# The order of PE's and ScalarE's steps within a chunk of an embedding tower: copies, within-double slots and layers moved

## The chip, the cores and the metric

One core of one Trainium2 chip runs the whole program in one launch. The metric is the device time in microseconds of one execution; of the kernel before three runs are at hand, and one further execution was recorded by the hardware profiler.

## The reference

For 2048 rows, 32 categorical fields are looked up in 32 tables (64 numbers each). Every pair of fields (496 pairs) goes through a bilinear form of its own, the 496 results through a linear layer of 256, and that with 16 dense numbers through three more layers:

```python
rows, cols = np.triu_indices(num_fields, k=1)
p = feat_emb[:, rows, :]
q = feat_emb[:, cols, :]
pij = jnp.einsum('bpe,dpe,bpd->bp', p, kernel, q)
z = pij @ W.T + b
h = jnp.concatenate([z, dense_ctx], axis=1)
h = jnp.maximum(h @ W_top1 + b_top1, 0.0)
h = jnp.maximum(h @ W_top2 + b_top2, 0.0)
y = h @ W_top3
```

All of it is float32.

## The kernel before, in words

The 2048 rows are worked on in four chunks of 512 columns (`CHUNKS`, numbered 0 to 3). The fields are taken two at a time as 16 "doubles": a double is 2 fields x 64 numbers = 128 partitions. `emb_t` holds the 16 doubles of one chunk, transposed, so that a row of the batch is a column.

GpSimd (POOL) gathers the table rows by indirect DMAs, eight for each double and chunk (L420). What PE (TensorE) does is written as one list of steps, `program()` (L202 to L233), which every engine walks through for its own part. The kinds of steps are:

- **turn** (L650): PE transposes gathered doubles into `bilinear` in PSUM; ScalarE (ACT) copies them to `emb_t` (L464, `turn_out`). From chunk 1 on two doubles are turned at a time. `TURNS` says after which slot of the chunk, `TURNS_EARLY` after which slot of the chunk before.
- **slot** (L669, 92 a chunk): the kernels of one double m against one double j times the columns of double m: 8 matmuls on quarter-height, half-width pieces of the array that work side by side (16 records in the profile, since a float32 matmul has two). VectorE (DVE) multiplies the result by double j (L575) into `prod`. Four slots of a chunk, `(3, None)`, `(7, None)`, `(11, None)` and `(15, None)`, hold the pairs *within* four doubles; their product takes four narrow instructions on DVE (L572). Here they are called within slots. They stand at the end of rows 3, 7, 11 and 15, that is as slots 6, 21, 44 and 91.
- **batch** (L685, 32 a chunk, a double m of 6 to 13 and a tile of 128 rows): the same with the batch on the partitions. DVE multiplies (L586) into `batch_prod`, a ring of 3, and ACT reduces it in two halves (**reduce**, L497 to L508), each half 8 ACTIVATE instructions with an accumulator read (L505). The halves are queued on ACT `REDUCE_LAG` = 2 and 4 steps behind their batch.
- **sum** (L710, 46 "quads" a chunk, each of two slots): PE adds the products over partitions into `sums`. Quads 0 to 31 are group 0, the rest group 1. After quad 31 ACT copies group 0 out of `sums` to `sums_sb` (`group_out`, L475), and quad 32 must wait for that copy (L715). **join** (L699) adds the reduced batches to group 1 at the chunk's end, which ACT copies too; then SyncE (SP) fetches the dense inputs into spare rows of `sums_sb` by 8 DMAs (L390).
- **layer** (L727, 7 a chunk): outputs 0 to 3 of the first dense layer (4 terms each; the linear layer of 256 has been folded into its weights), 4 and 5 of the second, 6 of the last. A term is one 128x128 weight block against 512 columns. ACT copies each with its bias and ReLU (L486, L490, L493). Layers of chunk i run amid the slots of chunk i+1: after slot 10 and every fourth slot behind it (`FIRST_LAYER`, `LAYER_EVERY`). Those of chunk 3 run at the very end.

PSUM has eight banks. Two hold `sums`; the other six are a ring of three pairs, `bilinear`. Slots, batches, turns and layers use a pair each in the order of the list; a step has to wait until the pair of the third use before it was read out by DVE or ACT (`ring_free`, L635). Batches run from slot 11 on, every 2.3 slots (chunk 0: from 17). In chunk 0, which has no layers, a double is turned two units ahead of its first use.

What PE, DVE and ACT each do within a chunk is thus fixed by one list, in which a step may stand behind others on its own engine that wait for something else.

## Time and profile before

| | |
|---|---|
| median of 3 runs | 823.51 us (820.65 to 825.17) |
| the profiled execution, its own time | 825.15 us |
| span of its instructions | 823.4 us |
| PE busy | 772.7 us (94%) |
| DVE busy | 623.8 us (76%) |
| ACT busy | 552.4 us (67%) |
| POOL busy | 472.0 us (57%), over by 630 us |
| mean granted TensorE clock | 0.99 |

A chunk is told by its steps: the first slot of chunks 0 to 3 starts on PE at 45.9, 213.8, 409.0 and 600.3 us, and the last slot of chunk 3 at 786.0 us. A row of the timeline merges instructions of one line that follow each other without a gap: its start, its length, and in brackets how long the engine stood idle before it and what ended that. Matmuls overlap, so the distance from one row's start to the next one's start is what a step costs, and the length is not.

### The profile page before, as it was taken

How to read it: one execution, taken by the hardware profiler on the slowest of the kernel's cores; microseconds unless marked ns; L12 is line 12 of the kernel's file. 1: busy time of each engine (PE TensorE's matmuls, PEld its weight loads, DVE VectorE, ACT ScalarE, POOL GpSimd, SP SyncE). 2: the span in 40 equal slices, each digit the busy share in tenths (PEclk: the TensorE clock that was granted, in tenths of full speed). 3: DMA queues.
4: the chain of work that ended last, by engine and by line, in shares of the span. 5: the costliest groups of instructions: out<-in, count | busy, mean ns of one | idle time of the engine just before them, and what ended most of it. 6: DMA issues, size and time to landing. Idle time of an engine off the chain costs nothing.

```text
span 823.4 us, 29630 instructions
## 1 busy us (share of the span) xinstructions
PE 772.7 (94%) x11784; PEld 284.5 (35%) x11784; DVE 623.8 (76%) x580; ACT 552.4 (67%) x4181; POOL 472.0 (57%) x502
## 2 busy tenths in 40 slices
PE   4988899999999999989999999998999999998978
PEld 1323233434333333333433333333343333332333
DVE  4487899999755669989866758997885568997930
ACT  0112799999616588999614768999813668999911
POOL 5777777777777777777777777777774000000000
PEclk9999999999999999999999999999999999999999
DMA  9911111111111111111111111111110000000000
GB/s 260 358 41 29 28 30 28 30 29 29 30 30 28 28 29 28 30 29 30 28 31 27 29 28 30 29 30 28 30 30 19 2 2 2 3 3 2 3 3 0
DMA packets 21681, 30.50 MB, mean 37 GB/s; under 512 B 10898, under 2 KB 11410, under 8 KB 20904
## 3 DMA queue, kind: packets, MB, share of 16 engines
q0 software_dynamic: 15872, 16.28, 10.3%
q1 hardware_dynamic: 3512, 9.58, 3.3%
q10 hardware_dynamic: 2160, 2.76, 1.3%
q8 instruction: 92, 1.51, 0.8%
q14 instruction: 45, 0.37, 0.2%
HBM read 28.58 MB, written 0.01 MB: 35 GB/s over the span
## 4 chain that ended last, share of the span: by engine, by line
PE 69%; ACT 11%; POOL 7%; DVE 6%; issue 5%; DMA 2%; SPq 0%; DVEq 0%; POOLq 0%
PE bilinear L679 27%; PE sums L721 14%; PE bilinear L747 11%; PE bilinear L693 10%; ACT batch_prod L505 10%; POOL emb L420 5%; PE bilinear L656 3%; DVE prod L572 3%; PE bilinear L610 2%; POOL emb_first L420 2%; DVE prod L575 2%; DMA sums_sb<-looked_ids 1%; DVE w_comb_sb L555 1%; PE sums L705 1%; DMA emb<-table,ids_sb 1%
## 5 line engine op out<-in xcount | busy, mean ns | idle before, releaser
L505 ACT ACTIVATE batch_prod<-batch_prod 128x64 f32<-128x64 f32 x2048 | 489.6, 243 | 21.2 <-DVE batch_prod L586 21.1
L575 DVE TENSOR_TENSOR prod<-bilinear,emb_t 128x1024 f32<-128x1024 f32 x352 | 415.9, 1218 | 81.4 <-PE bilinear L679 79.8
L420 POOL DMA_INDIRECT emb<-table,ids_sb x368 | 347.3, 944 | 112.1 <-issue 110.3
L505 ACT ACTIVATION_READ_ACCUMULATOR batch_prod<-batch_prod 128x1 f32 x2048 | 387.3, 189 | 0.0
L679 PE MATMUL bilinear<-emb_t,k_sb 64*32 64x512 f32 x5888 | 371.7, 595 | 6.8 <-DVE prod L572 4.8
L721 PE MATMUL sums<-prod,row_sel 64*32 64x512 f32 x2944 | 199.3, 596 | 9.8 <-ACT sums_sb L475 8.1
L586 DVE TENSOR_TENSOR batch_prod<-bilinear,emb_first 128x1024 f32<-128x1024 f32 x128 | 156.1, 1219 | 52.7 <-PE bilinear L693 51.7
L679 PEld LDWEIGHTS bilinear<-emb_t,k_sb 64*32 64x32 f32 x5888 | 108.5, 106 | 204.2 <-issue 137.7
L420 POOL DMA_INDIRECT emb_first<-table,ids_sb x128 | 124.1, 969 | 44.7 <-issue 37.6
L693 PE MATMUL bilinear<-k_sb,emb_t 64*32 64x512 f32 x2048 | 139.9, 601 | 0.0
L464 ACT ACTIVATE emb_t<-bilinear 128x1024 f32<-128x1024 f32 (+1 forms) x40 | 33.9, 848 | 97.8 <-PE bilinear L656 91.2
L721 PEld LDWEIGHTS sums<-prod,row_sel 64*32 64x32 f32 x2944 | 56.1, 108 | 116.1 <-issue 94.7
L747 PE MATMUL bilinear<-sums_sb,w_comb_sb 128*128 128x512 f32 x128 | 58.6, 603 | 7.1 <-DVE prod L572 4.4
L693 PEld LDWEIGHTS bilinear<-k_sb,emb_t 64*32 64x32 f32 x2048 | 40.4, 108 | 69.2 <-issue 52.3
L572 DVE TENSOR_TENSOR prod<-bilinear,emb_t 64x512 f32<-64x512 f32 x64 | 44.1, 689 | 10.2 <-PE bilinear L679 8.5
L486 ACT ACTIVATE h_sb<-bilinear,b_comb_sb 128x512 f32<-128x512 f32 x16 | 11.0, 688 | 59.3 <-PE bilinear L747 59.3
L747 PEld LDWEIGHTS bilinear<-sums_sb,w_comb_sb 128*128 128x128 f32 x128 | 23.2, 189 | 42.5 <-issue 28.1
L656 PE MATMUL bilinear<-ident,emb 128*128 128x128 f32 x184 | 26.3, 281 | 7.9 <-DMA emb<-table,ids_sb 6.4
L475 ACT ACTIVATE sums_sb<-sums 128x512 f32<-128x512 f32 x16 | 8.6, 587 | 33.7 <-PE sums L705 33.7
L610 PE MATMUL bilinear<-prod,batch_prod 100*32 100x512 f32 (+1 forms) x160 | 20.1, 668 | 11.8 <-DVE prod L541 11.8
L656 PEld LDWEIGHTS bilinear<-ident,emb 128*128 128x128 f32 x184 | 19.6, 141 | 31.9 <-DVE prod L575 11.5
L747 PE MATMUL bilinear<-h_sb,w_sb 128*128 128x512 f32 x64 | 29.3, 603 | 0.9 <-ACT h_sb L486 0.9
(29 smaller groups left out, 105.3 us busy)
## 6 DMA issues: line engine op xcount, KB each, us to landing
emb<-table,ids_sb POOLq DMA_INDIRECT x368, 2.5
emb_first<-table,ids_sb POOLq DMA_INDIRECT x128, 2.5
k_sb<-k_slots SPq DMA_DIRECT2D x2, 896.0 KB, 19.8
k_sb<-k_slots SPq DMA_DIRECT2D x1, 1600.0 KB, 23.1
k_sb<-k_slots SPq DMA_DIRECT2D x1, 1408.0 KB, 19.4
k_sb<-k_slots SPq DMA_DIRECT2D x1, 1088.0 KB, 16.8
sums_sb<-looked_ids SPq DMA_DIRECT2D x1, 1024.0 KB, 9.6
k_sb<-k_slots SPq DMA_DIRECT2D x1, 1024.0 KB, 26.5
```

The source lines that it names most:

```text
L420: nc.gpsimd.indirect_dma_start(fields_of(i, j, t)[:, f % 2, :], None, tables[f], bass.IndirectOffsetOnAxis(ap=ids_sb[:, start + t, f:f + 1 ...
L464: nc.scalar.activation(emb_t[:, j:j + several, 0:n], bilinear[:, bank:bank + several, 0:n], ACT.Copy).then_inc(s_emb_t, 1)
L505: last = nc.scalar.activation(products, products, ACT.Copy, accum_out=batch_sums[:, t, half, row + f:row + f + 1])
L572: last = nc.vector.tensor_tensor(prod[rows, at + half, 0:n], bilinear[rows, bank + half, 0:n], emb_t[by, double, 0:n], ALU.mult)
L575: last = nc.vector.tensor_tensor(prod[:, at:at + 2, 0:n], bilinear[:, bank:bank + 2, 0:n], emb_t[:, j:j + 1, 0:n].to_broadcast([P, 2, n]), ...
L586: nc.vector.tensor_tensor(batch_prod[:, use % BATCH_PRODS, :, :], bilinear[:, bank:bank + 2, :], first.to_broadcast([P, 2, COLS]), ALU.mul ...
L610: last = nc.tensor.matmul(bilinear[col:col + QUARTER, bank, :], tables_sb[0:parts, f, k, e:e + QUARTER], one_hot[0:parts, n % ONE_HOT_RING ...
L656: last = nc.tensor.transpose(bilinear[:, bank + n, t * P:(t + 1) * P], fields_of(i, j + n, t), ident[:])
L679: last = nc.tensor.matmul(bilinear[col:col + QUARTER, bank + row // EMB, 0:n], k_sb[row:row + EMB, operand, col:col + QUARTER], emb_t[row: ...
L693: last = nc.tensor.matmul(bilinear[col:col + QUARTER, bank + row // EMB, :], emb_t[row:row + EMB, m, t * P + col:t * P + col + QUARTER], k ...
L721: last = nc.tensor.matmul(sums[32 * b:32 * b + 32, half, 0:n], row_sel[rows, 31 - pos:63 - pos], prod[rows, at + b, 0:n], start=pos == 0, ...
L747: last = nc.tensor.matmul(bilinear[0:weights.shape[1], ring_bank("layer", i, k), 0:n], weights, x, start=term == 0, stop=term == LAYER_TER ...
```

## The change

The code of the steps stays, and so do their numbers: no slot, batch, sum or transpose is added or taken away. What changes:

- Within slots stand at places 4, 21, 38 and 88 of a chunk.
- In `program()` sums due now are queued ahead of reductions due now, and reductions are held back while the last quad of a group is about to come (`copy_near`). `REDUCE_LAG` is 3.
- Places of turns and batches: `TURNS`, `TURNS_EARLY`, `BATCH_FROM`. Layers of the chunk before stand after slots 5, 8, 18, 21, 25, 34 and 38 instead of 10, 14, 18, 22, 26, 30 and 34.
- A layer waits for each term's input by itself, not for all of them before the first.
- The layers of the last chunk no longer use the ring: each has a bank of its own, and the first two terms of outputs 0 to 3 (they need group 0 alone) are a step `begin` of their own, ahead of the terms that need group 1 and the dense inputs.

```diff
+WITHIN_PLACES = {3: 4, 7: 21, 11: 38, 15: 88}
+SLOTS = [(m, j) for m, j in OPERANDS if j is not None and (m not in BATCHED_ROWS_OF or j not in BATCH_DOUBLES)]
+for _m, _place in WITHIN_PLACES.items():
+    SLOTS.insert(_place, (_m, None))
...
-FIRST_LAYER = 10
-LAYER_EVERY = 4
-REDUCE_LAG = 2
-TURNS_EARLY = {84: 0, 87: 2, 90: 4}
-TURNS = {8: 6, 17: 8, 27: 10, 40: 12, 54: 14}
-FIRST_BATCH_FROM, FIRST_BATCH_EVERY = 17, 2.3
-BATCH_FROM, BATCH_EVERY = 11, 2.3
+REDUCE_LAG = 3
+REDUCE_HOLD = 1
+TURNS_EARLY = {82: 0, 88: 2, 91: 4}
+TURNS = {8: 6, 21: 8, 26: 10, 38: 12, 59: 14}
+LAYERS = (5, 8, 18, 21, 25, 34, 38)
+FIRST_BATCH_FROM, FIRST_BATCH_EVERY = 20, 2.2
+BATCH_FROM, BATCH_EVERY = 10, 2.3
+BEGUN_TERMS = HALVES
...
-        while reduces and reduces[0][0] <= at:
+        while sums and sums[0][0] <= at:
+            step = sums.pop(0)[1]
+            if step[0] == "join":
+                steps += [r for _, r in reduces if r[1] == step[1]]
+                reduces = [r for r in reduces if r[1][1] != step[1]]
+            steps.append(step)
+        copy_near = any(due <= at + REDUCE_HOLD and kind == "sum" and (n + 1) % GROUP_QUADS == 0
+                        for due, (kind, _, n) in sums)
+        while reduces and reduces[0][0] <= at and not copy_near:
             steps.append(reduces.pop(0)[1])
-        while sums and sums[0][0] <= at:
-            steps.append(sums.pop(0)[1])
     steps += [step for at, step in reduces] + [step for at, step in sums]
-    steps += [("layer", NCHUNKS - 1, k) for k in range(NOUTS)]
+    steps += [("begin", NCHUNKS - 1, k) for k in range(H1_OUTS)] + [("layer", NCHUNKS - 1, k) for k in range(NOUTS)]
...
+        def layer_bank(i, k):
+            return bilinear[:, k % (2 * RING) if i == NCHUNKS - 1 else ring_bank("layer", i, k), :]
...
+            def begin(i, k):
+                if k == 0:
+                    pe.wait_ge(s_prod, NCHUNKS * NSLOTS)
+                    pe.wait_ge(s_batch_prod, BATCHES_TO[NCHUNKS])
+                layer_terms(i, k, range(0, BEGUN_TERMS))
...
+            def layer_terms(i, k, terms):
+                n = cols(i)
+                for term in terms:
                     if k < H1_OUTS:
+                        pe.wait_ge(s_sums_out, i * NSUMS + term + 1)
                         if term == NSUMS - HALVES:
                             pe.wait_ge(s_dense, (i + 1) * (16 * 8))
...
                     elif k < H2_OUTS:
+                        pe.wait_ge(s_layer_out, i * NOUTS + term + 1)
```

Three places of the order, before and with the change. In the changed kernel the lines are other ones: L699 is the slot, L713 the batch, L741 the sum, L725 the join, L676 the turn, L783 a layer's term; on ACT L525 is the reduction, L484 the copy of a turn, L495 of a group, L506, L510 and L513 of a layer.

ACT in chunk 1, from the copy of layer output 6 of the chunk before (before: L493) to the copies after the join (before: L475 the second time); eight ACTIVATEs are one half reduction. Before:

```order
57 L493 ACTIVATE h_sb<-bilinear 1x512
58 L505 ACTIVATE batch_prod,batch_sums<-batch_prod 128x64 x40
59 L464 ACTIVATE emb_t<-bilinear 128x1024
60 L505 ACTIVATE batch_prod,batch_sums<-batch_prod 128x64 x96
61 L464 ACTIVATE emb_t<-bilinear 128x1024
62 L505 ACTIVATE batch_prod,batch_sums<-batch_prod 128x64 x96
63 L475 ACTIVATE sums_sb<-sums 128x512 x2
64 L505 ACTIVATE batch_prod,batch_sums<-batch_prod 128x64 x120
65 L464 ACTIVATE emb_t<-bilinear 128x1024
66 L505 ACTIVATE batch_prod,batch_sums<-batch_prod 128x64 x8
```

and with the change:

```order
52 L484 ACTIVATE emb_t<-bilinear 128x1024
53 L513 ACTIVATE h_sb<-bilinear 1x512
54 L525 ACTIVATE batch_prod,batch_sums<-batch_prod 128x64 x144
55 L484 ACTIVATE emb_t<-bilinear 128x1024
56 L525 ACTIVATE batch_prod,batch_sums<-batch_prod 128x64 x48
57 L495 ACTIVATE sums_sb<-sums 128x512 x2
58 L525 ACTIVATE batch_prod,batch_sums<-batch_prod 128x64 x112
59 L484 ACTIVATE emb_t<-bilinear 128x1024
60 L525 ACTIVATE batch_prod,batch_sums<-batch_prod 128x64 x32
```

Between the turn of doubles 14 and 15 and the copy of group 0, ACT has 6 half reductions instead of 12; behind the copy, up to the turn of doubles 0 and 1 of the next chunk, 14 instead of 15.

PE at the start of chunk 1, from the join of chunk 0 to its first layer. Before:

```order
154 L705 MATMUL sums<-ident,batch_sums 32x128 x32
155 L679 MATMUL bilinear<-emb_t,k_sb 32x512 x8
156 L721 MATMUL sums<-prod,row_sel 32x512 x8
157 L679 MATMUL bilinear<-emb_t,k_sb 32x512 x16
158 L721 MATMUL sums<-prod,row_sel 32x512 x8
159 L679 MATMUL bilinear<-emb_t,k_sb 32x512 x8
160 L656 MATMUL bilinear<-ident,emb 128x128 x8
161 L679 MATMUL bilinear<-emb_t,k_sb 32x512 x8
162 L721 MATMUL sums<-prod,row_sel 32x512 x8
163 L679 MATMUL bilinear<-emb_t,k_sb 32x512 x8
164 L747 MATMUL bilinear<-sums_sb,w_comb_sb 128x512 x4
```

and with the change:

```order
155 L725 MATMUL sums<-ident,batch_sums 32x128 x32
156 L699 MATMUL bilinear<-emb_t,k_sb 32x512 x8
157 L783 MATMUL bilinear<-sums_sb,w_comb_sb 128x512 x4
158 L741 MATMUL sums<-prod,row_sel 32x512 x8
159 L699 MATMUL bilinear<-emb_t,k_sb 32x512 x16
160 L741 MATMUL sums<-prod,row_sel 32x512 x8
161 L699 MATMUL bilinear<-emb_t,k_sb 32x512 x8
162 L676 MATMUL bilinear<-ident,emb 128x128 x8
163 L783 MATMUL bilinear<-sums_sb,w_comb_sb 128x512 x4
```

The first layer output stands one slot behind the join, where it stood eight steps and a turn behind; the second stands directly behind the turn.

PE at the end of the program, after the join of chunk 3, with what each instruction waits for. Before:

```order
1606 L747 MATMUL bilinear<-sums_sb,w_comb_sb 128x512 [waits s_sums_out,s_prod]
1607 L747 MATMUL bilinear<-sums_sb,w_comb_sb 128x512
1608 L747 MATMUL bilinear<-sums_sb,w_comb_sb 128x512 [waits s_dense]
1609 L747 MATMUL bilinear<-sums_sb,w_comb_sb 128x512
```

and with the change:

```order
1606 L783 MATMUL bilinear<-sums_sb,w_comb_sb 128x512 [waits s_sums_out,s_batch_prod,s_prod]
1607 L783 MATMUL bilinear<-sums_sb,w_comb_sb 128x512 [waits s_sums_out] x7
1608 L783 MATMUL bilinear<-sums_sb,w_comb_sb 128x512 [waits s_dense,s_sums_out]
1609 L783 MATMUL bilinear<-sums_sb,w_comb_sb 128x512 [waits s_sums_out]
```

Eight terms of group 0, two of each of four outputs, now stand ahead of the first term that waits for the dense inputs, instead of two.

## Rows read from the trace of the kernel before

**Rows 1.** The page: the span and the busy time of the engines
```profile
span 823.4 us, 29630 instructions
PE 772.7 (94%) x11784; PEld 284.5 (35%) x11784; DVE 623.8 (76%) x580; ACT 552.4 (67%) x4181; POOL 472.0 (57%) x502
```

**Rows 2.** Timeline of PE around quad 32 of chunk 1
```profile
361.47 1.06 PE L721 MATMUL sums<-prod,row_sel 64*32 64x512 f32 x16
...
364.05 1.06 PE L679 MATMUL bilinear<-emb_t,k_sb 64*32 64x512 f32 x16
367.64 1.09 PE L721 MATMUL sums<-prod,row_sel 64*32 64x512 f32 x16 [2.53 <-ACT sums_sb L475]
368.52 1.62 PE L679 MATMUL bilinear<-emb_t,k_sb 64*32 64x512 f32 x16
...
372.79 1.50 PE L679 MATMUL bilinear<-emb_t,k_sb 64*32 64x512 f32 x24
```

**Rows 3.** The timeline's group copy on ACT, and a run of reductions in the chain
```profile
366.53 1.05 ACT L475 ACTIVATE sums_sb<-sums 128x512 f32<-128x512 f32 x2
...
103.03 11.46 ACT batch_prod L505 x96
```

**Rows 4.** Windows: length, busy PE, PEld, DVE, ACT, POOL; clock; DMA
```profile
369.00:372.00 3.00, 3.00 (x40) 1.08 (x32) 1.23 (x1) 3.00 (x27) 2.39 (x3) 0.50 0.18 38
244.77:397.56 152.79, 147.74 (x2300) 53.00 (x2292) 122.56 (x110) 127.94 (x1005) 115.33 (x123) 0.99 0.15 29
```

**Rows 5.** Timeline around within slots 21 and 44, chunk 1, PE and DVE
```profile
267.85 1.06 PE L679 MATMUL bilinear<-emb_t,k_sb 64*32 64x512 f32 x16
270.31 3.70 PE L747 MATMUL bilinear<-sums_sb,w_comb_sb 128*128 128x512 f32 x8 [1.40 <-DVE prod L572]
...
325.84 1.09 PE L679 MATMUL bilinear<-emb_t,k_sb 64*32 64x512 f32 x16 [1.12 <-DVE prod L572]
...
267.46 2.80 DVE L572 TENSOR_TENSOR prod<-bilinear,emb_t 64x512 f32<-64x512 f32 x4
```

**Rows 6.** Timeline of PE from the join of chunk 1 to slot 11
```profile
415.43 1.96 PE L705 MATMUL sums<-ident,batch_sums 128*32 128x128 f32 x64
417.32 1.09 PE L679 MATMUL bilinear<-emb_t,k_sb 64*32 64x512 f32 x16
...
426.66 1.07 PE L679 MATMUL bilinear<-emb_t,k_sb 64*32 64x512 f32 x16
427.66 3.70 PE L747 MATMUL bilinear<-sums_sb,w_comb_sb 128*128 128x512 f32 x8
431.29 1.09 PE L679 MATMUL bilinear<-emb_t,k_sb 64*32 64x512 f32 x16
```

**Rows 7.** Timeline of PE: chunk 0, its join, start of chunk 1
```profile
101.77 0.63 PE L656 MATMUL bilinear<-ident,emb 128*128 128x128 f32 x4 [0.55 <-DMA emb<-table,ids_sb]
...
115.06 1.95 PE L679 MATMUL bilinear<-emb_t,k_sb 64*32 64x512 f32 x32 [0.60 <-ACT emb_t L464]
...
221.19 1.07 PE L705 MATMUL sums<-ident,batch_sums 128*32 128x128 f32 x31
...
231.53 0.66 PE L656 MATMUL bilinear<-ident,emb 128*128 128x128 f32 x4 [1.54 <-DMA emb<-table,ids_sb]
...
240.17 1.09 PE L679 MATMUL bilinear<-emb_t,k_sb 64*32 64x512 f32 x16
```

**Rows 8.** Timeline after the last slot: PE, and SP's queue
```profile
791.51 1.95 PE L705 MATMUL sums<-ident,batch_sums 128*32 128x128 f32 x64
794.76 1.95 PE L747 MATMUL bilinear<-sums_sb,w_comb_sb 128*128 128x512 f32 x4 [1.30 <-ACT sums_sb L475]
798.17 12.28 PE L747 MATMUL bilinear<-sums_sb,w_comb_sb 128*128 128x512 f32 x28 [1.45 <-DMA sums_sb<-dense_t]
819.30 1.88 PE L747 MATMUL bilinear<-sums_sb,w_sb 128*1 128x512 f32 x4 [0.87 <-ACT sums_sb L490]
...
794.65 2.30 SPq L390 DMA_DIRECT2D sums_sb<-dense_t  x8
```

More of the change, by code:

```diff
@@ L221, in program @@
                 steps.append(("turn", i + 1, (TURNS_EARLY[which], 2)))
-            k = (which - FIRST_LAYER) // LAYER_EVERY
-            if i > 0 and (which - FIRST_LAYER) % LAYER_EVERY == 0 and 0 <= k < NOUTS:
-                steps.append(("layer", i - 1, k))
+            if i > 0 and which in LAYERS:
+                steps.append(("layer", i - 1, LAYERS.index(which)))
         else:
             reduces += [(at + REDUCE_LAG * (half + 1), ("reduce", i, (*which, half))) for half in range(HALVES)]
-        while reduces and reduces[0][0] <= at:
+        while sums and sums[0][0] <= at:
[7 more added lines that the diff above has]
+        while reduces and reduces[0][0] <= at and not copy_near:
             steps.append(reduces.pop(0)[1])
-        while sums and sums[0][0] <= at:
-            steps.append(sums.pop(0)[1])
     steps += [step for at, step in reduces] + [step for at, step in sums]
-    steps += [("layer", NCHUNKS - 1, k) for k in range(NOUTS)]
+    steps += [("begin", NCHUNKS - 1, k) for k in range(H1_OUTS)] + [("layer", NCHUNKS - 1, k) for k in range(NOUTS)]
     return steps
 PROGRAM = program()
-RING_USES = [step for step in PROGRAM if step[0] in ("slot", "batch", "turn", "layer")]
+RING_USES = [step for step in PROGRAM
+             if step[0] in ("slot", "batch", "turn") or (step[0] == "layer" and step[1] < NCHUNKS - 1)]
 RING_USE = {step: n for n, step in enumerate(RING_USES)}
@@ L479, in layer_out @@
                 n = cols(i)
-                source = bilinear[:, ring_bank("layer", i, k), 0:n]
+                source = layer_bank(i, k)[:, 0:n]
                 act.wait_ge(s_layer, i * NOUTS + k + 1)
@@ L765, in _ @@
                     join(i)
+                elif kind == "begin":
+                    begin(i, which)
                 elif kind == "layer":
```

22 lines of the change are left out of this document (11 added, 11 removed).

## The prediction

> **What bounds the kernel now.** I read the page first, for the busy shares: PE is busy in 772.7 of 823.4 us [rows 1]. Work that only shifts between DVE and ACT gains nothing, and PE's own work does not change in number. So the question is how much of PE's time is waiting, and which of it goes. For that I read PE's timeline start to start. Three consecutive steps take 364.05 - 361.47 = 2.58 us, 0.86 us each, if nothing waits [rows 2]; slots, batches and sums cost all the same. Whatever a step takes beyond that is a wait, and the bracket names who ended it. The places priced below make some 9 us of such waits in a steady chunk. The timelines of ACT and DVE there show why they are so costly. A half reduction takes 11.46 / 6 = 1.91 us (16 instructions of 96), so a batch costs ACT 3.82 us [rows 3]. A batch comes every 2.3 slots, which cost PE 3.3 + 1.15 steps = 3.82 us. DVE needs 3.3 x 1.13 = 3.7 us for it, at the 1.13 us from product to product that the timeline shows and of which the narrow within product is the exception, 2.80 us [rows 5]. Where no layer lies between, the three engines are equal, and no delay of one is made good. Over the batches of chunk 1 ACT is busy in 127.94 of 152.79 us [rows 4].
>
> **The change part by part.** All gains are of PE's time, against the profiled execution (span 823.4, its own time 825.15 us, 1.6 above the median 823.51, well inside 820.65 to 825.17).
>
> *Copy of group 0.* Quad 32 starts at 367.64 instead of 364.05 + 0.86: 2.73 us [rows 2]. ACT reached the copy only at 366.53, for 12 half reductions stood ahead of it, though quad 31 was done near 362.5. The next three steps take 372.79 - 368.52 = 4.27 instead of 2.57 us: 1.70 us more [rows 2], and the granted clock there is 0.50, the 1.2 GHz level, after PE had stood idle 2.53 us [rows 4]. Together 4.43 us, in chunks 1, 2 and 3. With the change 6 half reductions stand ahead. I count in us from the start of the turn of doubles 12 and 13 (slot 38). PE: turn and layer 6 until 3.0, 41 steps, turn of 14 and 15 done at 39.4, then 14 steps, quad 31 done at 51.5, quad 32 due at 54.0. ACT: copy of layer 6 done at 3.6, 18 halves to 38.0, waits for the turn, its copy to 40.4, 6 halves to 51.9, group copy (1.05) to 53.0. It is in time by 1.0 us. Gain 3 x 4.43 = **13.3 us**. Late next is ACT: 14 halves to 79.7, the copy of doubles 0 and 1 to 80.7, and PE wants that bank at 80.9. The ring of 3 `batch_prod` buffers holds by the same count, by 0.1 to 1 us in each batch. So ACT lives with margins of tenths; what it costs lies between 0 and the 2.73 us given back in each chunk.
>
> *Within slots.* Before, the 2.80 us on DVE hit the third ring use behind: 270.31 - 267.85 - 1.00 = 1.46 us at slot 21, and 1.33 us at slot 44, of which the timeline brackets 1.12 as idle [rows 5]. At 21 and 38 a turn and a layer (1.05 + 3.63 or 1.9 us) now follow, on which DVE has nothing to do, and the third use comes after them. Gain 3 x 2.8 = **8.4 us**. For (15, None) at 88 the turn behind covers it but for 0.35 us at slot 90, about what slot 2 of the next chunk waited before: nothing. (3, None) lies under the layer behind the join.
>
> *Turn directly ahead of a layer.* A step ahead of a layer takes 1.00 instead of 0.86, and one behind it 0.88 [rows 6]. Three layers a chunk (8, 21, 38) now share that with a turn: 3 x 3 x 0.17 = **1.5 us**.
>
> *Layer 0 one slot behind the join.* It needs the dense inputs, which SP can fetch only once ACT has copied the join. At the end of the program they take from the join's start 798.17 - 791.51 = 6.66 us until PE goes on [rows 8]. With the change PE gets there after join 1.89, slot 0.86 + 0.14 and two terms 1.79 = 4.67 us: **a new wait of 2.0 us**. It hides the 0.42 us that sum 0 waited for the copy and DVE's backlog from the within slot. Before, slot 11 began 431.29 - 415.43 = 15.86 us behind the join [rows 6]; now the same steps end at 6.66 + 1.99 (two terms and restart) + 5 steps + turn 1.2 + 3 steps = 16.7. Loss 0.85 us in chunks 2 and 3: **-1.7 us**. The Trainium skill (DMA: Bandwidth & Descriptors, Anatomy of one DMA) gives a DMA a fixed cost of about 2.0 us; behind the last of eight issues [rows 8], which ends at 796.95, that would be 798.9, and the new wait 2.8 us. The row has 1.2 us there, and the sum goes by it.
>
> *Chunk 0 and start of chunk 1.* Until 101.77 PE waits for gathers [rows 7], at POOL's pace, so nothing is won. Behind it the changed order has one batch more to do (5 instead of 6 done). ACT had the turn of double 11 late (until 115.06 [rows 7], 0.83 us), and similar ones later, 2.7 us in all. In chunk 0 ACT is the bound: 57 halves from 103.0, 108.9, and 6.3 for copies end at 218.2, with its idle at double 11 about 219.3. Then the join, before at 221.19: **+1.8 us**. From there chunk 1 took 240.17 - 221.19 = 18.98 to slot 11, with a gather wait at 231.53 and the clock down behind it; now 16.7, as the turn comes at 232.5, after the gather: **+2.3 us**. If the join comes no earlier only the first goes.
>
> *End.* `begin` can start at 793.4, when the join's matmuls are out, instead of 794.76 + a wait to 798.17. 8 + 8 terms of 0.86 end at 807.2, before at 798.17 + 12.1 = 810.3 [rows 8]. Waiting term by term, output 4 needs no pause for the copy of output 3 (1.05 us), and the last layer's first term runs under the copy of output 5 (0.87). Sum 3.1 + 1.0 + 0.8 = **4.9 us**. The extra waits cost nothing: 28 records with a wait at every second term run without a gap, 0.43 us each [rows 8]. DVE ends chunk 3 as before: the same work stands behind slot 86.
>
> Sum: 13.3 + 8.4 + 1.5 - 1.7 + 1.8 + 2.3 + 4.9 = 30.5 us. From this I take 1.5 us for ACT's thin margins, towards the low end of 0 to 3 x 2.73, because the count fits everywhere. Gain 29.0: span 794.4, median 823.5 - 29.0 = **794.5 us**.
>
> **The rivals.**
> 1. *The wait moves.* ACT used the 4.4 us stall to catch up: it was 3 us behind before, and even after. If ACT arrives later at slot 38 than I count, or a half takes longer beside full DVE, the 2.73 us come back at the turn of doubles 0 and 1 or at the `batch_prod` ring, with the clock's 1.70. For it: margins of 0.1 us. Against: ACT idles 25 of 152.79 us [rows 4], most of it before slot 38. Given back whole, 13.3: 807.8 us.
> 2. *The new wait lowers the clock.* 2.0 us behind the join, where the array runs small matmuls, in three chunks. Behind idle 2.53 us the clock fell [rows 2, 4]; behind 1.40 it did not [rows 5]. Each fall costs 1.70 us as above: 3 x 1.7, so 799.6 us. The Trainium skill (TensorE: Matmul & The Clock Gate, Part 1) says the same, that idleness takes PE to half clock, and speaks against placing a wait there. At the program's end rows show the like, 1.30 and 1.45 us idle [rows 8], with terms behind at full pace.
> 3. *Slower: ACT becomes the bound of every chunk.* The place is the turn of doubles 0 and 1, at slot 82, after 38 halves since slot 38. To lose 30.5 us and more ACT must come 10 us too late in each of three chunks. That is 0.27 us on each half, 2.18 instead of 1.91 us; it decides from there. Then PE waits 10.5 us a chunk there, some 825 us, and 828 with the clock's falls. The halves are longer nowhere in the trace, though DVE and PE are full beside them.
> 4. *The order does not do what it says*: the reductions held back pile up ahead of the join. Against: the order shows them done by the third slot behind the last batches. It would cost 2 x 1.91 us a chunk: 806 us.
>
> **How the numbers follow.** My forecast has 0.60, with its own range 791 to 798. Rival 1 has 0.17 (800 to 810, as it may come in part), rival 2 0.14 (796 to 801), rival 4 0.04, rival 3 0.03; 0.02 is left for more gain than I count. The range reaches from 790.5, with no margin lost and a bit more from chunk 0, to 806, with most of rival 1. About 0.5% (4 us) is what a measurement of this kernel can tell from none. Only rival 3 is not faster by more: faster 0.95, same 0.02, slower 0.03.
>
> **What would show it.** Quad 32 three steps behind quad 31 with no bracket; no 0.50 clock in chunks 1 to 3; layers behind within slots starting without idle; a bracket of about 2 us for the dense DMA in each of three layers 0; one row of 16 terms at the end, the last layer 5 us nearer to the last slot. A first-slot-to-first-slot distance of 184 us in chunk 2, instead of 191.3, is right, 188 or more is wrong (rival 1), and brackets that name ACT at slot 84 or DVE's batch products say where.

## The result, and the profile after

The changed kernel takes 798.68 us (median of 6 runs, 796.73 to 799.11), the kernel before 823.55 us in the same session (6 runs, 820.65 to 825.17). The ratio is 0.9694, with a 95% interval from 0.9673 to 0.9716: faster by 24.9 us. Forecast were 794.5 us, within 790.5 to 806.0.

The profiled execution of the changed kernel was its fastest, 796.73 us. The page, beside [rows 1]:

```profile
span 794.9 us, 29641 instructions
PE 760.8 (96%) x11784; PEld 283.7 (36%) x11784; DVE 623.9 (78%) x580; ACT 551.3 (69%) x4181; POOL 472.3 (59%) x502
```

The work is the same, the span 28.5 us shorter. From profile to profile more was won than from median to median: the profiled execution of before lay 1.6 us above its median and that of after 1.95 us below. From join to join the profiles compare as follows. A chunk is counted from the join before it to its own; the end is what follows the join of chunk 3.

| | before | after | gain | forecast |
|---|---|---|---|---|
| start to join of chunk 0 | 221.2 | 222.5 | -1.3 | +1.8 |
| chunk 1 | 194.24 | 184.22 | 10.0 | 10.0 |
| chunk 2 | 191.28 | 184.03 | 7.25 | 6.9 |
| chunk 3 | 184.80 | 177.45 | 7.35 | 6.9 |
| end | 31.84 | 26.74 | 5.1 | 4.9 |

The forecasts by chunk are the prediction's terms added up where they fall: 4.43 + 2.8 + 0.5 + 2.3 for chunk 1, and 4.43 + 2.8 + 0.5 - 0.85 for chunks 2 and 3. They make 30.5 us; the 1.5 us of margin taken off stood in no chunk. From first slot to first slot chunk 2 took 184.0 us (400.6 to 584.6), the number that the prediction had named as its sign of being right.

**Quad 32.** The timeline of PE in chunk 1 of the changed kernel, from quad 31 (the first row) to quad 32 (the fourth), beside [rows 2]:

```profile
357.05 1.06 PE L741 MATMUL sums<-prod,row_sel 64*32 64x512 f32 x16
357.91 1.06 PE L713 MATMUL bilinear<-k_sb,emb_t 64*32 64x512 f32 x16
358.77 1.92 PE L699 MATMUL bilinear<-emb_t,k_sb 64*32 64x512 f32 x32
360.49 1.06 PE L741 MATMUL sums<-prod,row_sel 64*32 64x512 f32 x16
361.34 1.06 PE L713 MATMUL bilinear<-k_sb,emb_t 64*32 64x512 f32 x16
```

From start to start it is 3.44 us, four steps of 0.86: no wait, no bracket, and the granted clock from 357 to 362 us is 1.00. The distance was 367.64 - 361.47 = 6.17 us, with the same four steps.

**Within slots.** The timeline of PE around slot 21 of chunk 1, beside [rows 5]:

```profile
264.73 1.06 PE L699 MATMUL bilinear<-emb_t,k_sb 64*32 64x512 f32 x16
265.73 1.09 PE L676 MATMUL bilinear<-ident,emb 128*128 128x128 f32 x8
266.66 3.60 PE L783 MATMUL bilinear<-sums_sb,w_comb_sb 128*128 128x512 f32 x8
270.19 1.09 PE L699 MATMUL bilinear<-emb_t,k_sb 64*32 64x512 f32 x16
```

Turn, layer and next slot follow each other without idle; DVE's 2.8 us lie under them. The pair is also cheaper than the prediction counted. The turn takes 266.66 - 265.73 = 0.93 us and the layer behind it 270.19 - 266.66 = 3.53, where they take 1.02 and 3.63 apart; with the shared 0.17 that makes 0.36 us a pair instead of 0.17, at slots 8 and 21. It is most of the 0.4 us by which chunks 2 and 3 gained more than forecast.

**Layer 0.** The timeline of PE behind the join of chunk 0:

```profile
222.49 1.95 PE L725 MATMUL sums<-ident,batch_sums 128*32 128x128 f32 x64 [0.67 <-ACT batch_prod L525]
224.37 1.09 PE L699 MATMUL bilinear<-emb_t,k_sb 64*32 64x512 f32 x16
225.39 1.98 PE L783 MATMUL bilinear<-sums_sb,w_comb_sb 128*128 128x512 f32 x4
229.52 1.95 PE L783 MATMUL bilinear<-sums_sb,w_comb_sb 128*128 128x512 f32 x4 [2.14 <-DMA sums_sb<-dense_t]
231.40 1.09 PE L741 MATMUL sums<-prod,row_sel 64*32 64x512 f32 x16
```

The new wait is there, 2.14 us (1.84 and 1.98 in the next two chunks). With it the three chunks lose 2.59, 2.29 and 2.43 us on the layer beyond its bare terms. Of each of these 0.21 us are no wait: a layer that waits for nothing takes 3.63 us instead of 4 x 0.86. The clock did not fall behind this wait (window: length, busy PE, PEld, DVE, ACT, POOL; clock; DMA):

```profile
230.00:232.00 2.00, 2.00 (x20) 0.71 (x26) 0.00 (x0) 0.49 (x1) 1.39 (x3) 1.00 0.13 25
```

**End.** The timeline of PE from the join of chunk 3, beside [rows 8]:

```profile
768.19 1.95 PE L725 MATMUL sums<-ident,batch_sums 128*32 128x128 f32 x64
770.08 14.00 PE L783 MATMUL bilinear<-sums_sb,w_comb_sb 128*128 128x512 f32 x32
783.91 7.03 PE L783 MATMUL bilinear<-h_sb,w_sb 128*128 128x512 f32 x16
790.87 1.88 PE L783 MATMUL bilinear<-sums_sb,w_sb 128*1 128x512 f32 x4
```

Sixteen terms in one row of 32 records and no bracket: the dense inputs come while PE works on what needs none of them.

**Chunk 0** went the other way. Its timeline shows waits of PE behind the within slots at 38 and 88, where this chunk has no layer:

```profile
120.15 1.09 PE L699 MATMUL bilinear<-emb_t,k_sb 64*32 64x512 f32 x16 [1.27 <-DVE prod L592]
...
210.95 1.09 PE L713 MATMUL bilinear<-k_sb,emb_t 64*32 64x512 f32 x16 [0.86 <-DVE prod L592]
```

and ACT's timeline shows that ACT, which I had taken as the bound of this chunk, stands idle ahead of its copy of group 0 (the queue rule holds its reductions back there):

```profile
169.09 1.08 ACT L495 ACTIVATE sums_sb<-sums 128x512 f32<-128x512 f32 x2 [1.37 <-PE sums L741]
```

Even so ACT is the last at the end of this chunk: in the timeline above, the join at 222.49 us waits 0.67 us for a reduction of ACT.

### The profile page after: what moved, and what is told of

It is laid out like the page before. It is cut to its first block, busy times and chain, and to the rows that moved or that the text cites. A ratio compares the mean times of both kernels' runs of the same rounds, so it can differ in the third digit from the quotient of the medians.

```text
span 794.9 us, 29641 instructions
## 1 busy us (share of the span) xinstructions
PE 760.8 (96%) x11784; PEld 283.7 (36%) x11784; DVE 623.9 (78%) x580; ACT 551.3 (69%) x4181; POOL 472.3 (59%) x502
## 3 DMA queue, kind: packets, MB, share of 16 engines
q8 instruction: 92, 1.51, 0.8%
## 4 chain that ended last, share of the span: by engine, by line
PE 72%; POOL 9%; issue 6%; DVE 5%; ACT 5%; DMA 1%; SPq 1%; DVEq 0%; POOLq 0%
PE bilinear L699 30%; PE sums L741 16%; PE bilinear L713 12%; PE bilinear L783 11%; POOL emb L440 5%; ACT batch_prod L525 5%; POOL emb_first L440 4%; PE bilinear L676 3%; DVE prod L595 3%; DVE prod L592 1%; DVE batch_prod L606 1%; PE sums L725 1%; SPq L410 1%; DMA sums_sb<-dense_t 1%; ACT emb_t L484 0%
## 5 line engine op out<-in xcount | busy, mean ns | idle before, releaser
L525 ACT ACTIVATE batch_prod<-batch_prod 128x64 f32<-128x64 f32 x2048 | 489.2, 244 | 17.6 <-DVE batch_prod L606 17.6
L525 ACT ACTIVATION_READ_ACCUMULATOR batch_prod<-batch_prod 128x1 f32 x2048 | 389.9, 190 | 0.0
L699 PE MATMUL bilinear<-emb_t,k_sb 64*32 64x512 f32 x5888 | 368.1, 594 | 4.3 <-DVE prod L592 3.4
L741 PE MATMUL sums<-prod,row_sel 64*32 64x512 f32 x2944 | 196.8, 590 | 0.7 <-DVE prod L595 0.7
L699 PEld LDWEIGHTS bilinear<-emb_t,k_sb 64*32 64x32 f32 x5888 | 110.0, 107 | 207.1 <-issue 151.0
L713 PE MATMUL bilinear<-k_sb,emb_t 64*32 64x512 f32 x2048 | 137.1, 590 | 1.1 <-DVE prod L592 1.1
L484 ACT ACTIVATE emb_t<-bilinear 128x1024 f32<-128x1024 f32 (+1 forms) x40 | 34.0, 851 | 96.7 <-PE bilinear L676 90.0
L741 PEld LDWEIGHTS sums<-prod,row_sel 64*32 64x32 f32 x2944 | 55.9, 107 | 99.5 <-issue 92.0
L783 PE MATMUL bilinear<-sums_sb,w_comb_sb 128*128 128x512 f32 x128 | 58.5, 600 | 6.0 <-DMA sums_sb<-dense_t 6.0
L713 PEld LDWEIGHTS bilinear<-k_sb,emb_t 64*32 64x32 f32 x2048 | 39.0, 107 | 69.8 <-issue 48.8
L506 ACT ACTIVATE h_sb<-bilinear,b_comb_sb 128x512 f32<-128x512 f32 x16 | 11.0, 687 | 56.4 <-PE bilinear L783 56.4
L783 PEld LDWEIGHTS bilinear<-sums_sb,w_comb_sb 128*128 128x128 f32 x128 | 23.0, 190 | 36.5 <-issue 33.8
L676 PE MATMUL bilinear<-ident,emb 128*128 128x128 f32 x184 | 26.6, 284 | 3.9 <-DMA emb<-table,ids_sb 3.9
L676 PEld LDWEIGHTS bilinear<-ident,emb 128*128 128x128 f32 x184 | 19.9, 142 | 27.5 <-issue 12.6
L783 PE MATMUL bilinear<-h_sb,w_sb 128*128 128x512 f32 x64 | 29.2, 602 | 0.0
L495 ACT ACTIVATE sums_sb<-sums 128x512 f32<-128x512 f32 x16 | 8.6, 588 | 25.7 <-PE sums L725 24.3
```

Of the source, the lines that this page charges most:

```text
L484: nc.scalar.activation(emb_t[:, j:j + several, 0:n], bilinear[:, bank:bank + several, 0:n], ACT.Copy).then_inc(s_emb_t, 1)
L525: last = nc.scalar.activation(products, products, ACT.Copy, accum_out=batch_sums[:, t, half, row + f:row + f + 1])
L676: last = nc.tensor.transpose(bilinear[:, bank + n, t * P:(t + 1) * P], fields_of(i, j + n, t), ident[:])
L699: last = nc.tensor.matmul(bilinear[col:col + QUARTER, bank + row // EMB, 0:n], k_sb[row:row + EMB, operand, col:col + QUARTER], emb_t[row: ...
L713: last = nc.tensor.matmul(bilinear[col:col + QUARTER, bank + row // EMB, :], emb_t[row:row + EMB, m, t * P + col:t * P + col + QUARTER], k ...
L741: last = nc.tensor.matmul(sums[32 * b:32 * b + 32, half, 0:n], row_sel[rows, 31 - pos:63 - pos], prod[rows, at + b, 0:n], start=pos == 0, ...
```

## The experiments

**My theory** after the result: each part works as its term says; the order of ACT's queue removes quad 32's wait; the within slots' places, the layer's wait and `begin` are worth their terms; and chunk 0 lost because ACT is its bound and the batches begin three slots later. **The rivals**: the turn of doubles 14 and 15, moved from slot 54 to 59, removes quad 32's wait, and the queue rule does nothing; the clock falls behind layer 0's wait in most executions, so that the wait costs more than its length; chunk 0 lost to the within slots.

The twelve runs were made in three sessions, on three chips. Where a run is compared with the changed kernel's 798.68 us, that number is from the session of the result; the kernel before, within 0.3 us of the same median in the second and third session, is the link.

### First session: one part at a time

On the first chip the kernel before itself took 1339.5 us instead of 823.5. PE stands there waiting on nothing that the profile shows, as long as POOL gathers. The windows of the first experiment, before and after the last gather (it ends near 1090 us; columns as in [rows 4]):

```profile
792.80:1089.00 296.20, 255.97 (x2365) 85.94 (x2362) 124.39 (x112) 119.38 (x881) 121.68 (x129) 0.85 0.08 16
1132.00:1312.00 180.00, 174.97 (x2804) 63.53 (x2796) 146.13 (x133) 134.14 (x1040) 0.00 (x0) 1.00 0.01 3
```

Chunk 3, which lies behind the gathers, runs there as it does elsewhere, so I read chunk 3 of these four profiles alone, against 184.80 us of before and 177.45 us of after.

*The queue rule alone*, put on the kernel before, with its turns, within slots, layers and end:

```diff
-REDUCE_LAG = 2
+REDUCE_LAG = 3
+REDUCE_HOLD = 1
...
-        while reduces and reduces[0][0] <= at:
-            steps.append(reduces.pop(0)[1])
         while sums and sums[0][0] <= at:
...
+        copy_near = any(due <= at + REDUCE_HOLD and kind == "sum" and (n + 1) % GROUP_QUADS == 0
+                        for due, (kind, _, n) in sums)
+        while reduces and reduces[0][0] <= at and not copy_near:
+            steps.append(reduces.pop(0)[1])
```

> The kernel before with the new queue rule alone (sums ahead of reductions, reductions held back near a group's last quad, lag 3): in chunks 1 to 3 ACT has 10 half reductions instead of 12 between the turn of doubles 14 and 15 and the group copy. Theory A (the two halves taken from ahead of the copy are what removes the wait of quad 32): the copy starts 2 x 1.91 = 3.8 us earlier, near 362.7, just when quad 31 is done; quad 32 does not wait, the clock does not fall behind it: 3 x 4.43 = 13.3 us less, about 810 us. Theory B (ACT is behind as a whole, so that the wait moves to the next turn): quad 32 free, but a wait of 2 to 3 us ended by ACT at the turn of doubles 0 and 1: about 818 us.

Measured: 1340.57 us, ratio 1.0 (0.9956 to 1.0044), which says nothing on this chip. Chunk 3 took 180.33 us, 4.47 less than before, against the 4.43 that the prediction gave the term. Between the turn and the group copy this order has 10 half reductions, not 6, and quad 32 does not wait. So the rule suffices by itself.

*The rule off*, in the changed kernel:

```diff
-REDUCE_LAG = 3
-REDUCE_HOLD = 1
+REDUCE_LAG = 2
+REDUCE_HOLD = 0
...
-        while reduces and reduces[0][0] <= at and not copy_near:
+        while reduces and reduces[0][0] <= at:
             steps.append(reduces.pop(0)[1])
+        while sums and sums[0][0] <= at:
+            steps.append(sums.pop(0)[1])
```

> The changed kernel with the queue rule undone (reductions ahead of sums, no holding back, lag 2), all places of the change kept: 6 half reductions still stand between the turn of doubles 14 and 15 and the group copy, but 19 instead of 18 ahead of that turn. Theory A (the rule removes the wait of quad 32): the wait of 2.73 us and the clock's 1.70 us come back in chunks 1 to 3, about 812 us. Theory C (the later turn of doubles 14 and 15, at slot 59 instead of 54, does it, since ACT no longer idles 1.85 us ahead of it): ACT's copy of the turn is 0.5 us later, the group copy ends 0.5 us ahead of quad 32, no wait: 799 us within 1.5.

Measured: 1321.53 us, ratio 0.9867 (0.979 to 0.9944). Chunk 3 took 177.34 us, as with the rule, and quad 32 did not wait. So beside the other changes the rule does nothing in chunk 3.

*The turn alone*, in the kernel before:

```diff
-TURNS = {8: 6, 17: 8, 27: 10, 40: 12, 54: 14}
+TURNS = {8: 6, 17: 8, 27: 10, 40: 12, 59: 14}
```

> The kernel before with one number changed: doubles 14 and 15 are turned after slot 59 instead of 54. Theory A (the queue rule alone matters): as before, 823.5 us. Theory C: ACT does not idle 1.85 us ahead of that turn, the group copy comes 1.85 us earlier in chunks 1 to 3, quad 32 waits 0.9 instead of 2.73 us and the clock may stay up: 3 x 1.85 = 5.5 us, and 3 x 1.70 = 5.1 us if it does, 813 us (818 if it falls all the same).

Measured: 1341.75 us, ratio 1.0012 (0.9965 to 1.0059). Chunk 3 took 181.27 us, 3.53 less; from quad 31 to quad 32 it is 4.34 us, of which 0.9 is a wait. The later turn removes most of the wait too, and the clock's fall with it. Both parts do the same thing, and they do not add.

*The within slots back*, in the changed kernel:

```diff
-WITHIN_PLACES = {3: 4, 7: 21, 11: 38, 15: 88}
+WITHIN_PLACES = {3: 6, 7: 21, 11: 44, 15: 91}
```

> The changed kernel with the within slots back at 6, 21, 44 and 91. My sum gave 1.33 us for slot 44 in each of chunks 1 to 3 and nothing for 6 and 91; slot 21 keeps its place beside turn and layer. So 4 us slower, 802.7 us, with an idle of about 1.1 us ended by DVE two uses behind slot 44. Rival (the wait given to DVE's backlog at slots 88 and 4 in the changed kernel, 0.45 to 1.1 us, is worth as much): about as the changed kernel, 799 us. Chunk 0 should gain 1.5 us at slot 38, where no layer covers the within slot, if ACT is not the bound there.

Measured: 1317.7 us, ratio 0.9862 (0.9795 to 0.9928). Chunk 3 took 179.6 us, 2.15 more. It lost 1.92 us at quad 44, behind the within slot at its very end, where the changed kernel lost 0.75 + 0.92 us at slot 90 and quad 44, and five pieces of 0.3 to 0.7 us around the other two. Of the new places, these three are tried; slot 21 keeps its place in both kernels.

### Second session: the end, layer 0, and chunk 0

The kernel before took 823.28 us on this chip (7 runs, 821.97 to 824.19).

*No `begin`*, in the changed kernel:

```diff
-    steps += [("begin", NCHUNKS - 1, k) for k in range(H1_OUTS)] + [("layer", NCHUNKS - 1, k) for k in range(NOUTS)]
+    steps += [("layer", NCHUNKS - 1, k) for k in range(NOUTS)]
...
-                    terms = range(BEGUN_TERMS, LAYER_TERMS[k])
+                    if k == 0:
+                        pe.wait_ge(s_prod, NCHUNKS * NSLOTS)
+                        pe.wait_ge(s_batch_prod, BATCHES_TO[NCHUNKS])
+                    terms = range(LAYER_TERMS[k])
```

> The changed kernel without the begin steps: the last chunk's layers do all four terms of an output before the next; the waits term by term stay. Theory (my sum): the dense inputs land 6.66 us behind the join's start, PE has two terms (1.79 us) to do until then and waits about 2.8 us instead of none: 3.0 us slower than the changed kernel, 801.7 us. Rival (the gain at the end comes from waiting term by term and from the join's copy no longer being waited for by all terms): the same as the changed kernel within 1 us.

Measured: 802.90 us, ratio 0.9757 (0.9738 to 0.9776). The end took 29.8 us instead of 26.74, 3.06 more. The forecast was 3.0 us more than the changed kernel, 801.7. Its timeline:

```profile
770.50 1.95 PE L725 MATMUL sums<-ident,batch_sums 128*32 128x128 f32 x64
772.38 1.98 PE L786 MATMUL bilinear<-sums_sb,w_comb_sb 128*128 128x512 f32 x4
777.20 12.26 PE L786 MATMUL bilinear<-sums_sb,w_comb_sb 128*128 128x512 f32 x28 [2.83 <-DMA sums_sb<-dense_t]
```

The wait of 2.83 us is back ahead of the 28 records. The other 5.1 - 3.06 = 2.0 us of the end's gain stay without `begin`: they come from the waits term by term and the banks of their own, which this kernel keeps; the two were not taken apart. By medians it is 4.2 us slower. In its profile chunk 1 took 186.00 us, 1.8 more than in that of after, with the clock down in layer 0 behind 2.11 us of idle (clock 0.53 over the window from 229.7 to 233.3 us).

*Layer 0 later*, in the changed kernel:

```diff
-LAYERS = (5, 8, 18, 21, 25, 34, 38)
+LAYERS = (7, 8, 18, 21, 25, 34, 38)
```

> The changed kernel with layer output 0 after slot 7 instead of 5. Theory (the wait for the dense inputs is PE's own loss): the wait of 2.0 to 2.1 us in each of chunks 1 to 3 goes, sum 0 waits 0.42 us for the join's copy instead: 3 x 1.6 = 4.8 us faster than the changed kernel, 793.9 us. Rival (the wait only hides DVE's backlog from the within slot at 4): waits ended by DVE come at slot 6 or the turn behind it, and the time stays at 798.7.

Measured: **791.56 us** (791.18 to 792.24), ratio 0.9619 (0.9603 to 0.9635): 7.1 us less than the changed kernel. Its timeline behind the join of chunk 1:

```profile
404.62 1.96 PE L725 MATMUL sums<-ident,batch_sums 128*32 128x128 f32 x64
406.50 1.09 PE L699 MATMUL bilinear<-emb_t,k_sb 64*32 64x512 f32 x16
407.78 1.09 PE L741 MATMUL sums<-prod,row_sel 64*32 64x512 f32 x16 [0.19 <-ACT sums_sb L495]
408.66 1.93 PE L699 MATMUL bilinear<-emb_t,k_sb 64*32 64x512 f32 x32
410.52 3.70 PE L783 MATMUL bilinear<-sums_sb,w_comb_sb 128*128 128x512 f32 x8
```

Three steps later, the layer's four terms (8 records) run without a break, and quad 0 waits only 0.19 us for the copy (0.42 us from start to start). Chunks 1 to 3 took 182.39, 182.38 and 175.65 us: 1.8, 1.65 and 1.8 us less each, 5.3 us in the profiles. The remaining 1.8 of the 7.1 us is the distance of the profiled execution of after from its median, less 0.4 us for the one here. It is about the price of one fall of the clock. The profile of after has none behind layer 0, but it is the fastest of six executions; one more is at 797.0, and four lie at 798.4 to 799.1, some 2 us higher. That these four had a fall there is not shown: the mean granted clock is 0.996 in all six, the fastest too.

*The batches of chunk 0 back*, in the changed kernel:

```diff
-FIRST_BATCH_FROM, FIRST_BATCH_EVERY = 20, 2.2
+FIRST_BATCH_FROM, FIRST_BATCH_EVERY = 17, 2.3
```

> The changed kernel with chunk 0's batches from slot 17 every 2.3 slots, as before. Theory (ACT is the bound of chunk 0 behind the last gather wait, and has 2 half reductions more left there since the batches start later): join of chunk 0 up to 3.0 us earlier than 222.5, 2.5 to 3 us faster than the changed kernel, 796 us. Rival (the within slot at 38, uncovered in chunk 0, or POOL's gathers set the join of chunk 0 and the turn behind it at 231.5): the same as the changed kernel.

Measured: 798.44 us (797.35 to 800.15), ratio 0.9696 (0.9677 to 0.9714), no change. The join of chunk 0 stands at 223.9 us, 1.4 later, and ACT, which should have been the bound, idles 8.3 us amid its line: 0.90, 0.44, 1.72, 1.38, 0.85, 1.29 and 1.70 us. The 1.4 us went to a wait behind quad 36, 2.29 us, which the changed kernel does not have. The next step, slot 76, is the first that needs double 15. PE turned it by 183.5 us, but ACT stood in its reductions until 186.79. PE's timeline and ACT's:

```profile
184.32 1.06 PE L741 MATMUL sums<-prod,row_sel 64*32 64x512 f32 x16
187.47 1.95 PE L699 MATMUL bilinear<-emb_t,k_sb 64*32 64x512 f32 x32 [2.08 <-issue]
186.79 0.57 ACT L484 ACTIVATE emb_t<-bilinear 128x512 f32<-128x512 f32 x1
```

The bracket says "issue", but PE goes on 0.11 us behind the end of that copy (187.36). The queue rule alone shows the same in its profile: copy done at 185.59, slot 76 at 185.69, 1.91 us idle. So with the earlier batches ACT is behind at double 15, and PE waits for it there. **That the later batches cost chunk 0 its time falls**; that ACT can hold PE up in this chunk does not. The profile also shows something else. The timeline and the windows behind the join of chunk 0:

```profile
226.82 1.98 PE L783 MATMUL bilinear<-sums_sb,w_comb_sb 128*128 128x512 f32 x4
231.03 3.58 PE L783 MATMUL bilinear<-sums_sb,w_comb_sb 128*128 128x512 f32 x4 [2.23 <-DMA sums_sb<-dense_t]
```

```profile
231.00:234.00 3.00, 2.97 (x4) 1.17 (x4) 0.00 (x0) 0.00 (x0) 2.39 (x3) 0.50 0.15 30
```

Here the clock did fall behind the wait, to 1.2 GHz: the same four records take 3.58 us that took 1.95 in the changed kernel's profile, and the layer loses 4.31 us, against 2.59. Of the four executions, two took 797.35 and 797.55 us with a mean granted clock of 0.998, and two 799.33 and 800.15 with 0.996. So a fall is worth about 2 us, and whether it comes differs from execution to execution. It differs within this profile too: in chunk 2 layer 0 waited longer, and its terms ran at full pace.

```profile
417.10 1.96 PE L783 MATMUL bilinear<-sums_sb,w_comb_sb 128*128 128x512 f32 x4 [2.29 <-DMA sums_sb<-dense_t]
```

*Both*, layer 0 later and the batches back:

> The changed kernel with both: layer output 0 after slot 7 and chunk 0's batches from slot 17. If the two gains are in different places they add: 4.8 + 2.8 = 7.6 us faster than the changed kernel, 791 us; but in chunk 1 the turn of doubles 6 and 7 would then come up near 227.5 us, ahead of its gathers (231.5), so that there the gains up to that point do not add: 793 us.

Measured: 792.32 us (791.57 to 793.13), ratio 0.9623 (0.9606 to 0.9639). That is layer 0's gain and nothing beside it; the join of chunk 0 stands at 223.9 us again. That 793 us was nearly met is luck: it counted on a gain in chunk 0 that a gather would take back, and there was no such gain.

### Third session: what adds and what doesn't, on a chip that can be read whole

The kernel before took 823.46 us here (7 runs, 822.07 to 825.06). The first two kernels are those of the first session, *the queue rule alone* and *the turn alone*:

> The kernel before with the new queue rule alone, once more: on the first chip the trace could be read in chunk 3 only, where quad 32 did not wait and the chunk was 4.5 us shorter. If all three chunks behave so: 13.3 us less than before, 810 us, join to join 186.8 us in chunk 2. If the wait comes back at the turn of doubles 0 and 1, which chunk 3 does not have: 818 us.

> The kernel before with the turn of doubles 14 and 15 at slot 59, once more: in chunk 3 on the first chip quad 32 waited 0.9 us, the clock stayed up, and the chunk was 3.5 us shorter. If all three chunks behave so: 10.6 us less than before, 813 us, with no half clock in chunks 1 to 3. If the queue rule alone matters: 823 us.

Measured: 810.69 us for the rule (ratio 0.9846, 0.9828 to 0.9864), 12.8 less than before; 813.48 us for the turn (0.9884, 0.9864 to 0.9905), 10.0 less. The two timelines of PE in chunk 1 from quad 31 to quad 32, the rule first:

```profile
359.97 1.06 PE L729 MATMUL sums<-prod,row_sel 64*32 64x512 f32 x16
...
362.54 1.06 PE L687 MATMUL bilinear<-emb_t,k_sb 64*32 64x512 f32 x16
363.40 1.06 PE L729 MATMUL sums<-prod,row_sel 64*32 64x512 f32 x16
```

and the turn:

```profile
360.21 1.06 PE L721 MATMUL sums<-prod,row_sel 64*32 64x512 f32 x16
...
362.79 1.06 PE L679 MATMUL bilinear<-emb_t,k_sb 64*32 64x512 f32 x16
364.54 1.09 PE L721 MATMUL sums<-prod,row_sel 64*32 64x512 f32 x16 [0.69 <-ACT sums_sb L475]
```

3.43 and 4.33 us, where it was 6.17. In chunks 1 to 3 no other wait took the place of the one removed, and neither profile has a half clock there. Both kernels keep the waits behind the within slots of before (1.60 to 1.65 at slot 22 and 1.33 to 1.51 at slot 45 with the rule), so these are a cost of their own.

*The rule off beside layer 0 later*: the edit of the second experiment, on the fastest kernel.

> Layer output 0 after slot 7, and the queue rule undone (reductions ahead of sums, lag 2). If the rule is not needed once the turn stands at slot 59 and the chunks are without other waits: join to join 182.4 us in chunk 2 as with it, and in chunk 0 ACT no longer idles 1.37 us ahead of its group copy, so 0 to 1.4 us less than with the rule: 790.2 to 791.6 us. If the rule is what keeps quad 32 free: 4.4 us a chunk more, 805 us.

Measured: 793.84 us (793.3 to 794.18), ratio 0.9642 (0.9624 to 0.9659), 2.3 more than with the rule. Chunks 1 to 3 took 182.47, 182.33 and 175.65 us, as with it. Neither value forecast came: the rule is not needed for quad 32 in chunks 1 to 3, but it is worth something in chunk 0. All of the difference lies ahead of the join of chunk 0, at 224.3 us instead of 222.2. Its timeline of PE has three waits for ACT that the kernel with the rule lacks: 0.84 us for the copy of double 11, 1.13 us for that of double 15, and the group copy's:

```profile
172.81 1.09 PE L735 MATMUL sums<-prod,row_sel 64*32 64x512 f32 x16 [0.98 <-ACT sums_sb L489]
```

Some 0.9 of their 3.2 us come back at the join, which no longer waits for ACT.

So in the full change the new places, the later turn above all, do the work in chunks 1 to 3 (the turn alone left 0.9 us of wait), and the rule in chunk 0, which has turns of one double and at other places.

*The within slots back beside layer 0 later*: the edit of the fourth experiment, on the fastest kernel.

> Layer output 0 after slot 7, and the within slots back at 6, 21, 44 and 91. From chunk 3 of the first such run, 1.1 us behind slot 44 and 1.1 us behind slot 6, with about the same at slots 91 to 2, each in chunks 1 to 3: 2.2 to 3 us a chunk, 6.5 to 9 us; less 1.3 us if the wait behind slot 38 in chunk 0 was PE's own loss: 797 to 799 us. If within slots in chunk 0 only share ACT's bound, its join stays at 222 us and nothing comes back: 798 to 800 us.

Measured: 794.37 us (793.99 to 794.55), ratio 0.9647 (0.963 to 0.9665), 2.8 more, where 5.4 to 7.4 more was forecast. Chunks 1 to 3 took 183.87, 183.87 and 176.97 us, which is 1.48, 1.49 and 1.32 more, 4.3 together; but chunk 0 was done sooner: its join stands at 220.71 us, 1.5 earlier than the fastest kernel's and 0.5 earlier than the one of before.

The new places of the within slots gain in chunks with layers and lose in the one without.

## Why the prediction was right, and where it was not

*Copy of group 0, 13.3 us: right, in size and in mechanism.* The rule alone brought 12.8 us by medians and 4.47 us in the one chunk read on the first chip. What I did not see is that two parts of the change each remove most of it alone, 12.8 and 10.0 us, and that they don't add. My count from slot 38 ran through both at once and could not tell them apart. In chunks 1 to 3 neither margin was needed: 10 half reductions were as good as 6.

*Within slots, 8.4 us: right for what can be told.* Half of that term was slot 44, 3 x 1.33 = 4.0 us. Moving it and its fellows was worth 4.3 us in chunks 1 to 3. Against that stand 1.5 us lost in chunk 0, which the term did not have, so by the runs these three places were worth 2.8 us net. The other half, slot 21, shows in the timeline of after as a stretch without idle; it was not tried by itself, nor were the 1.5 us of turns placed ahead of layers, which by the timeline were undercounted (0.36 us a pair at slots 8 and 21).

*Layer 0, -1.7 us by a new wait of 2.0 us: right in the wait.* It was 2.14, 1.84 and 1.98 us, and 2.4, 2.1 and 2.2 us were lost beyond the 0.21. The net of 0.85 us a chunk was not measured by itself; moving the layer two slots back won 1.8, 1.65 and 1.8 us. The other price named, 2.8 us, worked out from the Trainium skill (DMA: Bandwidth & Descriptors, Anatomy of one DMA), is more than any of the three show; the section's figure is for a DMA that GpSimd issues, and these are issued by SyncE. (The 2.83 us at the end without `begin` are another count: no slot stands there between join and layer. From the join's start to the end of the wait it is 777.20 - 770.50 = 6.70 us, as in [rows 8].)

*Rival 2, the clock falls behind the new wait: came true in part.* It did not fall in the profile of after, where the idle was 2.14 us, but did in two others of this order, in chunk 1 alone: behind 2.23 us without the late batches and behind 2.11 us without `begin`. A fall cost 4.31 - 2.59 = 1.7 us, of which the wait itself was 0.1 longer, the size that [rows 2] gave. I had made it a case of three falls or none; in the profiles it was one or none of three, and not the same in each execution. That the four executions of after at 798.4 to 799.1 us owe their 2 us to such a fall is what the experiment with the batches back suggests. Their traces were not recorded, and their mean clock of 0.996 is that of the fastest too, whose two half-clock stretches before the end lie in chunk 0, near 44 and 82 us. So it stays open. With the wait gone the kernel was 7.1 us faster, of which 5.3 are the waits. The Trainium skill (TensorE: Matmul & The Clock Gate, Part 1) says that idleness takes PE to half clock; the two profiles with 0.50 and 0.53 behind the wait agree, and the profile of after, with 1.00 behind 2.14 us, shows that it need not.

*End, 4.9 us: right.* 5.1 us, 3.06 of them by `begin`, for which the prediction had 3.1, and 2.0 by the rest, for which it had 1.8.

*Start of chunk 1, +2.3 us: right for this profile, and mostly luck.* Chunk 1 gained 2.8 us more than chunk 2, where the term and the absent 0.85 us made 3.15. But the 18.98 us from join to slot 11, from which the term was worked out, held one fall of the clock. The profiles of the rule alone and of the turn alone, with the same order there, have waits of 1.23 and 1.51 us for the gather, no fall, and take 17.16 and 17.25 us. So about 1.8 of the 2.3 us was a fall that need not come. It is also about the 1.6 us by which the profiled execution lay above its median: the mean clock was 0.990 in it, and 0.992 in ten of the fourteen executions of the later sessions. That the two are the same thing is likely and not shown.

*Rivals 1, 3 and 4 did not come.* Quad 32's wait came back nowhere, ACT bound none of chunks 1 to 3, and nothing piled up ahead of a join. So the 1.5 us that I took off for ACT's margins were given for nothing.

**The step that failed** is "In chunk 0 ACT is the bound: 57 halves from 103.0, 108.9, and 6.3 for copies end at 218.2, with its idle at double 11 about 219.3. Then the join, before at 221.19: +1.8 us." It gave -1.3, an error of 3.1 us, larger than all but three of the terms. The term that was mis-sized is ACT's idle: 219.3 - 218.2 = 1.1 us were allowed for it, and ACT waited 0.90, 0.39, 1.37 and 1.19 us in that stretch, 3.85 in all. 218.2 + 3.85 = 222.05; ACT's last reduction ended at 222.43, and the join, which waits for it, stands at 222.49. So ACT was the last, as I had said; a sum of one engine's work is its end only if it never waits. I had priced the within slots in the three chunks with layers and left out chunk 0, where nothing covers them: 1.48 us lost at slot 39 and 1.07 at slot 89. Put back at their old places they give 1.5 us of the 3.1. The batches' later start gives none of it, and without the queue rule chunk 0 would have lost another 2.1 us. The rest was in the count too: with the within slots back ACT still waited 0.87 us for a turn and 1.47 us ahead of its group copy, and 218.2 + 2.34 = 220.5 us. Its last reduction ended at 220.66 and the join stood at 220.71, not at 219.4.

So the profiles' terms miss by little: 30.5 forecast, less 3.1 in chunk 0, plus 1.0 in chunks 2 and 3 and the end, make 28.4, and I had forecast 29.0 after the 1.5 us of margin that nothing took. The forecast of 794.5 us was 4.2 below the median; 3.6 of it is that the profiled execution of before was 1.6 us slow, and that of after 1.95 us fast, each against its median; the other 0.6 is the terms. I had named the first number and still subtracted a gain worked out on that execution from the median.

## What to carry to other kernels

When a change reorders several queues, price every moved step once in each stage that has another set of covers: a step that hides under a layer in three chunks stands bare in the one without layers, and the sum of an engine's work is no end as long as that engine waits for others. When a bracket names no engine ("issue"), look at what the next step needs and when it was done. Two edits that both free the same wait do not add; count which of them is already enough. A term worked out from a stretch in which the clock fell is worth what it says only in executions with that fall. And a wait of some 2 us on TensorE deserves to be moved away, as it may take the clock with it: one number, `LAYERS` from 5 to 7, was worth 7.1 us here, and 791.56 us is the fastest kernel of the study.
